# Attention probabilities in tiles of 4 heads by 32 queries, turned by VectorE, with score matmuls on four 64x64 quadrants

## The chip, the core and the metric

The kernel runs on one core of a Trainium2 chip. The metric is device time in microseconds (us), the median of several executions. Five engines work from queues of their own, each in its written order, and signal each other by semaphores: TensorE (PE, matmuls; PEld is its weight load), VectorE (DVE), ScalarE (ACT), GpSimd (POOL) and SyncE (SP), which here only issues DMAs.

## The reference, cut to what matters

The program is one transformer-like layer over 32 sequences of 128 tokens with 128 channels, in fp32. A mixture of 8 experts with a shared one feeds an attention with a band of 32 (no softmax), a layer norm and a residual. Then comes the attention that the change touches: 16 heads of 64 channels that share one key and one value, l2-normalised queries and keys, a learnt relative bias, a causal mask, a padding mask and one "null" key. A gated feed-forward network ends it.

```
q  = l2norm(xn @ Wq) * q_scale            # 16 heads x 64
k, v = split(xn @ Wkv)                    # one head of 64, shared
s  = 8 * q @ [null_k, l2norm(k) * k_scale].T + [null_bias, rel_bias + causal + padding]
p  = softmax(s)                           # 128 queries x (1 + 128) keys
z  = (p @ [null_v, v]) @ Wout             # then a layer norm and the feed-forward part
```

Key positions after the query are masked with -1e30, so their probabilities are zero.

## The kernel before, in words

The 32 sequences go in 8 groups of 4 (`GB`). A pass works on three groups at once: stage A of group g+1 (routing, experts, band attention, norms, projection of q, k and v), stage B of group g (the attention with softmax), and stage C of group g-1 (feed-forward). The passes are fill, start, five of "steady", seventh, last and drain. The order of each engine's work in a pass is a table written out by hand (`ORDER`, lines 53 to 193); each item is a step and its number, such as `sim.0`.

Stage B of one group, before:

- `sim.n` (PE, `sim`, L1369), 12 bursts, 3 for each sequence of 6, 6 and 4 heads: q of one head (64 x 128) times the keys (64 x 129), two heads at once on the upper and the lower 64 rows of the array, into two PSUM banks of ring S. A fp32 matmul shows as two records.
- `sim.n` on DVE (`score`, L1131): one instruction a head, 128 x 129, scales by 1/|q| (`rq`) and adds the masked bias. `max.j` (L1139), `ex.j` (ACT, L759), `inv.j` (L1144) and `pn.j` (POOL, L660) follow, with j = 0 to 15 for 4 heads each. `bias.j` (POOL, L653) makes the masked bias of 4 heads.
- `PT.j` (PE, `p_turn`, L1377): four 128x128 transposes into ring T, `PT.j` (ACT, `pt_copy`, L773) copies them to `pT`.
- `PV.n` (PE, `pv`, L1384), 8 a group: v (128 x 64) times the turned probabilities of 4 heads (128 x 512), twice, on the left and the right half of the columns. `PV.n` on ACT (`ot_copy`, L780) copies to `oT`, and `z.n` (PE, L1397) projects.

Stage A ends with the query norms: `qs.c` (PE, `q_sum`, L1351) sums the squares, `ssq` and `ssc` (DVE, with a PE transpose `qst` between them, L1358) bring them to rows, and `qn` (POOL, L643) takes the power -0.5, once for each sequence. `vs` (DVE, L1084) makes v minus the null value.

PSUM has ring M of 3 banks for stages A and C, S of 2, T of 2, and one bank for z.

SP's queue of a steady pass is `rw.0 maskn.0 wb.0 l4.0`: load the x of the next group (`load_x`, `xg` at L549 and `xs` at L551), its mask, the routing weights of the group after (`load_weights`, 8 DMAs, L542, once `l4` of PE has read `hA`), and store a group's result. ACT's and DVE's lists of a pass begin with `xh.0` (L718) and `xl.0` (L1016), which split x into a high and a low part; PE's `exp.0` to `exp.4` (L1255 by way of the helper `three`, L1243) are the first to read them. Then come `down.0` (L1296), `qkv.0` and so on.

## Time and profile before

| | |
|---|---|
| median of 3 runs | 814.14 us (812.65 to 814.35) |
| profiled execution, first to last instruction | 811.5 us |
| PE busy | 777.8 us, 96% |
| PE weight load busy | 593.4 us, 73% |
| ACT, DVE busy | 602.6 us (74%), 581.3 us (72%) |
| POOL busy | 460.3 us (57%) |
| DMA | 23.41 MB, mean 29 GB/s |

The profile gives no time of the execution beyond its span; the median lies 2.6 us above the span. A busy share tells how full an engine is; who sets the end is read from the chain of waits (from the last instruction back to what released it) and from the timeline. Matmul records overlap, so the time that a stretch of matmuls costs is read from the starts, or from the chain, not from the mean of a record. A steady pass takes 93.2 to 93.4 us.

### The profile page before, as it was taken

The numbers are of one execution on the slowest core, as the hardware profiler recorded it, in microseconds if no ns is written. First come the engines' busy times: TensorE is split into PE (matmuls) and PEld (weight loads), VectorE is DVE, ScalarE is ACT, GpSimd is POOL, SyncE is SP. The second block draws the span as 40 slices with busy tenths as digits, with TensorE's granted clock in tenths as the row PEclk, the third lists the DMA queues.
The fourth block names the chain that finished last, engine by engine and source line by source line (L and its number), as shares of the span: only waits on it lengthen the run. The fifth ranks groups of instructions, "written<-read, shape, count | busy, mean of one in ns | idle before, by whom it ended". The sixth has DMA issues, their size and how long they took to land.

```text
span 811.5 us, 16623 instructions
## 1 busy us (share of the span) xinstructions
PE 777.8 (96%) x5322; PEld 593.4 (73%) x5322; DVE 581.3 (72%) x1575; ACT 602.6 (74%) x1647; POOL 460.3 (57%) x388
## 2 busy tenths in 40 slices
...
DMA packets 28917, 23.41 MB, mean 29 GB/s; under 512 B 2192, under 2 KB 26400, under 8 KB 28448
## 3 DMA queue, kind: packets, MB, share of 16 engines
...
q14 instruction: 40, 0.33, 0.1%
...
## 4 chain that ended last, share of the span: by engine, by line
PE 68%; DVE 13%; POOL 7%; issue 5%; ACT 1%; DVEq 0%; POOLq 0%; ACTq 0%
PE ps_M L1243 33%; PE ps_S L1369 6%; PE ps_T L1384 6%; PE ps_z L1397 5%; PE ps_T L1377 5%; DVE sb_sm L1131 5%; PE ps_M L1429 3%; PE ps_M L1296 3%; POOL sb_sm L660 2%; PE ps_S L1351 2%; POOL sb_biasm L653 2%; DVE sb_hT L1043 2%; POOL sb_rq L643 1%; PE ps_M L1326 1%; DVE sb_bs L1033 1%
## 5 line engine op out<-in xcount | busy, mean ns | idle before, releaser
L660 POOL TENSOR_TENSOR sb_sm<-sb_sm,sb_rden 128x512 f32<-128x512 f32 x128 | 146.2, 1145 | 155.6 <-DVE sb_rden L1144 155.6
L759 ACT ACTIVATE sb_sm<-sb_sm,sb_nmx 128x129 f32<-128x129 f32 x512 | 200.1, 397 | 28.4 <-DVE sb_nmx L1139 28.0
L653 POOL TENSOR_TENSOR sb_biasm<-sb_bias,sb_maskn 128x512 f32<-128x512 f32 x128 | 168.8, 1326 | 57.3 <-DVE sb_sm L1131 36.7
L1131 DVE SCALAR_TENSOR_TENSOR sb_sm<-ps_S,sb_rq,sb_biasm 128x129 f32<-128x129 f32 x512 | 141.0, 345 | 24.0 <-PE ps_S L1369 20.1
L643 POOL TENSOR_TENSOR sb_rq<-sb_qss,sb_mhalf 128x16 f32<-128x16 f32 x32 | 93.2, 2938 | 21.9 <-DVE sb_qss L1116 21.9
L759 ACT ACTIVATION_READ_ACCUMULATOR sb_sm<-sb_sm,sb_nmx 128x1 f32 x512 | 99.1, 193 | 0.0
L1369 PEld LDWEIGHTS ps_S<-sb_k,sb_qs 64*128 64x128 f32 x1024 | 65.2, 187 | 40.7 <-issue 38.4
L773 ACT ACTIVATE sb_pT<-ps_T 128x512 f32<-128x512 f32 x128 | 74.8, 593 | 26.8 <-PE ps_T L1377 26.8
L1139 DVE TENSOR_REDUCE sb_nmx<-sb_sm 128x4 f32<-128x516 f32 x128 | 86.2, 682 | 1.4
L1369 PE MATMUL ps_S<-sb_k,sb_qs 64*128 64x129 f32 x1024 | 83.0, 291 | 3.8 <-DVE sb_sm L1131 2.2
L1377 PE MATMUL ps_T<-sb_ident,sb_sm 128*128 128x128 f32 x512 | 77.1, 276 | 3.7 <-POOL sb_sm L660 3.5
L1377 PEld LDWEIGHTS ps_T<-sb_ident,sb_sm 128*128 128x128 f32 x512 | 59.6, 141 | 22.4 <-POOL sb_sm L660 10.7
L1397 PE MATMUL ps_z<-sb_wout,sb_oT 128*128 128x128 f32 x512 | 66.9, 276 | 0.0
L1384 PE MATMUL ps_T<-sb_pT,sb_vs 128*64 128x512 f32 x256 | 64.9, 610 | 0.0
L1397 PEld LDWEIGHTS ps_z<-sb_wout,sb_oT 128*128 128x128 f32 x512 | 62.8, 192 | 2.7 <-issue 0.8
L1090 DVE TENSOR_SCALAR sb_qs<-ps_M,sb_cols 128x512 f32<-128x512 f32 x62 | 45.4, 745 | 23.2 <-ACT sb_hT L747 16.9
L1243 PE MATMUL ps_M<-sb_hAh,sb_h1h 128*128 128x512 f32 (+1 forms) x144 | 56.2, 390 | 1.1 <-DVE sb_hAl L959 0.9
L1243 PE MATMUL ps_M<-sb_hBh,sb_h2h 128*128 128x512 f32 (+1 forms) x144 | 55.9, 388 | 0.5 <-DVE sb_hBl L959 0.5
L1144 DVE RECIPROCAL sb_rden<-sb_den 128x4 f32<-128x4 f32 x128 | 21.8, 171 | 46.5 <-ACT sb_sm L759 46.4
L713 ACT ACTIVATE sb_gs<-ps_M 128x512 f32<-128x512 f32 x39 | 23.2, 595 | 41.2 <-PE ps_M L1243 41.1
L1243 PE MATMUL ps_M<-sb_hAh,sb_h1l 128*128 128x512 f32 (+1 forms) x144 | 53.2, 370 | 0.0
L1243 PE MATMUL ps_M<-sb_hAl,sb_h1h 128*128 128x512 f32 (+1 forms) x144 | 53.2, 369 | 0.0
...
## 6 DMA issues: line engine op xcount, KB each, us to landing
...
sb_xg<-in_xT SPq DMA_DIRECT2D x8, 256.0 KB, 4.1
sb_xs<-in_x SPq DMA_DIRECT2D x8, 256.0 KB, 4.6
sb_qs<-in_xT SPq DMA_DIRECT2D x1, 2048.0 KB, 10.2
sb_hA<-in_h SPq DMA_DIRECT2D x2, 1024.0 KB, 5.2
out_y<-sb_res SPq DMA_DIRECT2D x7, 256.0 KB, 3.9
sb_sm<-toeplitz SPq DMA_DIRECT2D x1, 1024.0 KB, 5.8
...
```

The costliest lines, as they stand in the source:

```text
L643: pool.tensor_tensor(rq[:, cut], qss[:, cut], mhalf[:], ALU.pow).then_inc(q_rnorm.sem, 1)
L653: pool.tensor_tensor(biasm[:, heads, 1:NK], bias0[:, heads], maskn[:, j // 4].unsqueeze(1).broadcast_to([128, 4, S]), ALU.add)\
L660: pool.tensor_tensor(sm[:, heads, 1:NK], sm[:, heads, 1:NK], rden[:, heads].unsqueeze(2).broadcast_to([128, 4, S]), ALU.mult)\
L759: ins = act.activation(sm[:, h], sm[:, h], ACT.Exp, bias=nmx[:, h:h + 1], accum_out=den[:, h:h + 1])
L773: act.activation(pT[:, heads].rearrange("p h s -> p (h s)"), bank(g, "PT", j)[:], ACT.Copy)\
L1131: ins = dve.scalar_tensor_tensor(sm[:, h], bank(g, "sim", n, odd)[:, m * NK:(m + 1) * NK], rq[:, k * HEADS + h:k * HEADS + h + 1], biasm[: ...
L1139: dve.tensor_reduce(nmx[:, heads], sm[:, heads], AX, ALU.max, negate=True).then_inc(max_ready.sem, 1)
L1243: ins = pe.matmul(ps, w[i], x[j], start=start and n == 0, stop=stop and n == 2)
L1369: ins = pe.matmul(ps[odd][:, m * NK:(m + 1) * NK], qs[half, lo + m, k * S:(k + 1) * S], k2[half, k], start=True, stop=True)
L1377: ins = pe.transpose(ps[:, h * S:(h + 1) * S], sm[:, j % 4 * 4 + h, 1:NK], ident[:])
L1384: ins = pe.matmul(ps[DH * odd:DH * (odd + 1)].rearrange("p (h s) -> p h s", h=4), vs[:, n // 2], pT[:, n % 2 * 8 + odd:n % 2 * 8 + 8:2], s ...
L1397: ins = pe.matmul(zbank[:, k * D:(k + 1) * D], oT[:, c], wout[:, c], start=(c == 0), stop=(c == NP - 1))
```

## The change

It touches stage B and what feeds it.

- Scores are tiled as 4 heads x 32 queries = 128 partitions. A query block i (0 to 3) needs keys up to 32(i+1) only, so tiles are 33, 65, 97 and 129 wide (`WIDE`); `sim`, the bias, the maxima, the exponentials, the division and the PV product skip the masked keys beyond. Units come in the order of `BLOCKS` 0, 3, 1, 2, two to a burst; there are 2 bursts a sequence instead of 3.
- `sim.n` (PE) issues 16 matmuls a burst of 64 rows x 64 columns, over the four quadrants of the array (`half` and `part`), instead of 6 or 4 of 64 rows x 128 columns.
- The PE transposes `PT`, their copies on ACT and ring T go. `tp.j` on DVE (`p_turn`) turns the probabilities in 32x32 blocks, straight into `pT`.
- After such a turn a column holds (head, key) pairs of four heads, so PV multiplies with `vblk`, a block form of v: rows of a 32-key block repeated for 4 heads, 64 rows of the array for a pair of heads, 128 columns. 14 matmuls a sequence of 256 or 128 columns stand for 4 of 512.
- `vblk` is filled by 16 DMAs a group on SP (`vb.0`, `spread_values`), which wait until `vs` is made and until the last PV of the group before has read the old one.
- The query norms are summed in 8 matmuls of 512 columns, turned by DVE from PSUM (the transpose `qst` goes).
- The first bias load from DRAM is 16 DMAs instead of one, and 4 small ones come before the expert weights.
- PSUM: ring S has 4 banks, shared by `sim`, `qs` and PV. All order tables are new.

```diff
-BURSTS = ((0, 3), (3, 6), (6, 8))
-NB = len(BURSTS)
-LAST_BURST = (0, 1, 1, 2)
+QW = 32
+BLOCKS = (0, 3, 1, 2)
+PAIRS = (BLOCKS[0:2], BLOCKS[2:4])
+NB = len(PAIRS)
+WIDE = [QW * (i + 1) + 1 for i in range(4)]
+TURNED = 5 * 128
+RING = 3
...
     "sp steady": """
-        rw.0 maskn.0 wb.0 l4.0
+        rw.0 maskn.0 wb.0 l4.0 vb.0
     """,
...
-BANKS = {"M": 3, "S": 2, "T": 2}
+BANKS = {"M": 3, "S": 4}
...
+            def spread_values(g, k):
+                sp.wait_ge(v_shifted.sem, v_shifted.at(g, 1))
+                if g == 0:
+                    sp.wait_ge(v_cleared, 1)
+                sp.wait_ge(pv_psum.sem, pv_psum.at(g, 0))
+                for i in range(4):
+                    for c in range(4):
+                        sp.dma_start(vblk[c * QW:(c + 1) * QW, :, i, c % 2 * DH:(c % 2 + 1) * DH], vs[i * QW:(i + 1) * QW])\
+                            .then_inc(v_spread.sem, 16)
...
+            def p_turn(g, j):
+                n, (i, wide, _) = j // 2, unit(j % 4)
...
+                dve.wait_ge(p_normed.sem, p_normed.at(g, j + 1))
+                dve.wait_ge(pv_psum.sem, pv_psum.at(g, n + 1 - RING))
+                p = scored(g, j)[:, :, 1:wide].rearrange("p t (c k) -> p t c k", k=QW)
+                turned = pT[:, (g * GB * NB + n) % RING].rearrange("p (c t k) -> p t c k", t=4, k=QW)
+                if i == 2:
+                    dve.transpose(turned[:, :, 1:4:2], p[:, :, 0:2])
+                    ins = dve.transpose(turned[:, :, 4:5], p[:, :, 2:3])
...
             def sim(g, n):
-                k, (lo, hi) = n // NB, BURSTS[n % NB]
...
-                        ins = pe.matmul(ps[odd][:, m * NK:(m + 1) * NK], qs[half, lo + m, k * S:(k + 1) * S],
-                                        k2[half, k], start=True, stop=True)
+                for i in PAIRS[n % NB]:
+                    for m in range(2):
+                        for c in range(2):
+                            for odd in range(2):
+                                half, part = slice(64 * odd, 64 * odd + 64), slice(64 * c, 64 * c + 64)
+                                ins = pe.matmul(ps[odd][part, first:first + WIDE[i]],
+                                                qs[half, m, 4 * k + i, 2 * c:2 * c + 2].rearrange("p c q -> p (c q)"),
+                                                k2[half, k, 0:WIDE[i]], start=True, stop=True)
...
             def pv(g, n):
...
-                for odd in range(2):
-                    ins = pe.matmul(ps[DH * odd:DH * (odd + 1)].rearrange("p (h s) -> p h s", h=4), vs[:, n // 2],
-                                    pT[:, n % 2 * 8 + odd:n % 2 * 8 + 8:2], start=True, stop=True)
+                for c in range(hi + 1):
+                    both = c <= lo
+                    for r in range(2):
+                        half = slice(64 * r, 64 * r + 64)
...
+                        src = pT[half, ring, first:first + (256 if both else 128)]
+                        ins = pe.matmul(dst, vblk[half, k, c], src, start=(c == 0), stop=(c == hi), skip_group_check=True)
```

Where things now stand. SP's queue between two steady passes, first before and then after: `sb_xg` and `sb_xs` are the x of the next group, `in_mask` its mask.

```order
L542 DMA sb_hA<-routes 64x4x128 x8
L566 DMA out_y<-sb_res 128x4x128
L549 DMA sb_xg<-in_xT 128x512
L551 DMA sb_xs<-in_x 128x4x128
L558 DMA sb_mask<-in_mask 128x512
```

```order
L567 DMA sb_hA<-routes 64x4x128 x8
L601 DMA out_y<-sb_res 128x4x128
L594 DMA sb_vblk<-sb_vs 32x4x64 x16
L574 DMA sb_xg<-in_xT 128x512
L576 DMA sb_xs<-in_x 128x4x128
```

Sixteen DMAs that wait for the last PV of the group now stand between the store and the load of x.

PE's queue over the same boundary, from the last PV (L1384, L1440) to the first matmul that reads the new x (`sb_xh`), first before: L1358 turns the sums of squares, L1397 is z, L1369 the scores.

```order
L1384 MATMUL ps_T<-sb_pT,sb_vs 64x512 x2
L1358 MATMUL ps_S<-sb_ident,sb_ssT 128x128
L1397 MATMUL ps_z<-sb_wout,sb_oT 128x128 x8
L1369 MATMUL ps_S<-sb_k,sb_qs 128x129 x6
L1243 MATMUL ps_M<-sb_xh,sb_wguh 128x512
```

The same of the changed kernel: L1453 is z, L1377 a transpose of k, L1402 the sums of squares, L1416 the scores.

```order
L1440 MATMUL ps_S<-sb_pT,sb_vblk 128x256 x4
L1440 MATMUL ps_S<-sb_pT,sb_vblk 128x128 x2
L1453 MATMUL ps_z<-sb_wout,sb_oT 128x128 x4
...
L1453 MATMUL ps_z<-sb_wout,sb_oT 128x128 x4
L1377 MATMUL ps_M<-sb_ident,sb_hT 128x128 x4
L1402 MATMUL ps_S<-sb_hT,sb_heads 32x512 x2
L1402 MATMUL ps_S<-sb_gs,sb_heads 32x512 x2
L1453 MATMUL ps_z<-sb_wout,sb_oT 128x128 x12
L1416 MATMUL ps_S<-sb_k,sb_qs 64x33 x8
L1416 MATMUL ps_S<-sb_k,sb_qs 64x129 x8
L1416 MATMUL ps_S<-sb_k,sb_qs 64x65 x8
L1416 MATMUL ps_S<-sb_k,sb_qs 64x97 x8
L1294 MATMUL ps_M<-sb_xh,sb_wguh 128x512
```

What is left out in the middle are the nine matmuls of `q.5` to `q.7`. Before, one burst of scores stood between the last z and the experts; now two do.

## Rows read from the trace of the kernel before

**Rows 1.** Page, part 1: busy us, share of span, instructions.
```profile
PE 777.8 (96%) x5322; PEld 593.4 (73%) x5322; DVE 581.3 (72%) x1575; ACT 602.6 (74%) x1647; POOL 460.3 (57%) x388
```
**Rows 2.** Busy by stretch: start pass, a steady pass, last pass; header names the columns.
```profile
core 0: us, PE busy (x) PEld busy (x) DVE busy (x) ACT busy (x) POOL busy (x), PEclk, DMA share, GB/s
72.50:143.70 71.20, 63.93 (x484) 45.04 (x483) 60.35 (x162) 54.37 (x176) 57.20 (x43) 1.00 0.13 39
330.40:423.60 93.20, 91.98 (x629) 69.84 (x630) 69.13 (x185) 72.34 (x200) 56.98 (x45) 1.00 0.08 22
702.40:811.50 109.10, 103.04 (x730) 84.75 (x728) 54.87 (x147) 89.34 (x226) 36.76 (x35) 1.00 0.03 8
```
**Rows 3.** Chain of waits, 300 to 420 us: start, us, engine, line, records.
```profile
309.65 0.72 PE ps_S L1369 x8
...
323.38 0.44 PE ps_T L1377 x4
...
324.25 0.89 PE ps_z L1397 x8
325.14 0.71 PE ps_M L1243 x3
...
326.29 1.01 PE ps_S L1351 x32
327.30 1.01 PE ps_T L1384 x4
328.31 0.26 PE ps_S L1358
...
330.36 0.87 PE ps_S L1369 x12
...
340.71 4.53 PE ps_M L1296 x10
...
357.81 1.87 PE ps_T L1384 x8
```
**Rows 4.** Timeline of SP in the fill and at a pass boundary.
```profile
4.68 0.43 SPq L494 DMA_DIRECT2D sb_pb<-in_pb  x1
5.15 0.42 SPq L494 DMA_DIRECT2D sb_maskn<-in_wqkv  x1
5.62 0.44 SPq L506 DMA_DIRECT2D sb_xs<-in_x  x1
...
36.90 0.33 SPq L515 DMA_DIRECT2D toeplitz<-sb_pT  x1
38.35 0.38 SPq L517 DMA_DIRECT2D sb_sm<-toeplitz  x1
...
410.97 5.20 SPq L542 DMA_DIRECT2D sb_hA<-routes  x8
416.22 0.86 SPq L566 DMA_DIRECT2D out_y<-sb_res  x1
417.12 0.50 SPq L549 DMA_DIRECT2D sb_xg<-in_xT  x1
```
**Rows 5.** DMA issues: KB each, us from issue to landing.
```profile
sb_xg<-in_xT SPq DMA_DIRECT2D x8, 256.0 KB, 4.1
sb_sm<-toeplitz SPq DMA_DIRECT2D x1, 1024.0 KB, 5.8
sb_maskn<-in_wqkv SPq DMA_DIRECT2D x1, 192.0 KB, 5.5
```
**Rows 6.** Timeline of ACT and DVE where a steady pass begins.
```profile
422.14 0.62 ACT L718 ACTIVATE sb_xh<-sb_xg 128x512 fp32r<-128x512 f32 x1
...
422.80 0.69 DVE L1016 TENSOR_TENSOR sb_xl<-sb_xg,sb_xh 128x512 fp32r<-128x512 f32 x1 [0.43 <-ACT sb_xh L718]
425.17 1.65 DVE L1131 SCALAR_TENSOR_TENSOR sb_sm<-ps_S,sb_rq,sb_biasm 128x129 f32<-128x129 f32 x6 [0.27 <-POOL sb_rq L643]
432.48 0.69 DVE L1139 TENSOR_REDUCE sb_nmx<-sb_sm 128x4 f32<-128x516 f32 x1
435.73 0.68 DVE L1002 TENSOR_TENSOR sb_hT<-ps_M,sb_gs 128x512 f32<-128x512 f32 x1
```
**Rows 7.** Timeline of PE in the fill: an idle stretch and the same matmuls after it.
```profile
53.42 0.66 PE L1281 MATMUL ps_M<-sb_ident,sb_hA 128*128 128x128 f32 x2 [4.30 <-DVE sb_hT L1043]
53.87 3.62 PE L1237 MATMUL ps_S<-sb_sm,sb_pT 128*128 128x512 f32 x4
...
58.99 0.61 PE L1326 MATMUL ps_M<-sb_ident,sb_hT 128*128 128x128 f32 x4
...
60.33 1.02 PE L1237 MATMUL ps_S<-sb_sm,sb_pT 128*128 128x512 f32 x2
```
**Rows 8.** Instructions of DVE, ACT by line and shape: busy us, mean ns, idle.
```profile
L1162 DVE SCALAR_TENSOR_TENSOR sb_al<-ps_M,sb_cols,sb_al 128x512 f32<-128x512 f32 x28 | 21.0, 751 | 14.6 <-ACT sb_al L794 11.8 <-PE ps_M L1243 2.8
L1162 DVE SCALAR_TENSOR_TENSOR sb_al<-ps_M,sb_cols,sb_al 128x256 f32<-128x256 f32 x8 | 3.9, 482 | 4.8 <-ACT sb_al L794 4.4 <-PE ps_M L1243 0.3
L773 ACT ACTIVATE sb_pT<-ps_T 128x512 f32<-128x512 f32 x128 | 74.8, 593 | 26.8 <-PE ps_T L1377 26.8
```
**Rows 9.** Timeline of DVE in the fill and where the start pass begins.
```profile
5.18 0.54 DVE L858 TENSOR_TENSOR sb_pT<-sb_condT,sb_wgT 64x256 f32<-64x256 f32 x1 [3.06 <-DMA sb_wgT<-in_wgT]
...
71.23 0.41 DVE L1084 TENSOR_TENSOR sb_vs<-sb_hT,sb_rows 128x256 f32<-128x256 f32 x1
...
74.99 1.65 DVE L1131 SCALAR_TENSOR_TENSOR sb_sm<-ps_S,sb_rq,sb_biasm 128x129 f32<-128x129 f32 x6 [0.78 <-POOL sb_rq L643]
```
**Rows 10.** POOL instructions by line and shape: busy us, mean ns, idle.
```profile
L653 POOL TENSOR_TENSOR sb_biasm<-sb_bias,sb_maskn 128x512 f32<-128x512 f32 x128 | 168.8, 1326 | 57.3 <-DVE sb_sm L1131 36.7 <-DVE sb_maskn L1097 20.5
L660 POOL TENSOR_TENSOR sb_sm<-sb_sm,sb_rden 128x512 f32<-128x512 f32 x128 | 146.2, 1145 | 155.6 <-DVE sb_rden L1144 155.6
L643 POOL TENSOR_TENSOR sb_rq<-sb_qss,sb_mhalf 128x16 f32<-128x16 f32 x32 | 93.2, 2938 | 21.9 <-DVE sb_qss L1116 21.9
```

More of the change, by code:

```diff
@@ L70 @@
+        mix.0 z.0 l3.0-2 sim.6-7 xnT.0 l3.3 z.1 kv.0 q.0-1 PV.2-4 q.2-3 l4.0 q.4 z.2 PV.5 qs.0-3 PV.6-7 z.3
+        q.5-7 z.4 kT.0 qs.4-7 z.5-7
     """,
     "pe seventh": """
-        exp.0 sim.0 exp.1-2 sim.1 exp.3 sim.2 exp.4 down.0 zT.0 PT.0 sim.3 PT.1 qkv.0 l1.0-1 PT.2 l1.2-3 sim.4
-        PV.0 scores.0 PT.3 sim.5 l2.0 PT.4 z.0 PT.5 sim.6 mix.0 PV.1 sim.7 PT.6 l2.1 PT.7 PV.2 sim.8 l2.2 PT.8
-        z.1 PT.9 z.2 sim.9 l2.3 PT.10 xnT.0 PV.3 sim.10 l3.0 kv.0 q.0 PT.11 q.1 sim.11 PV.4 q.2-3 l3.1 z.3 PT.12
@@ L138 @@
-        max.7 inv.6 sim.6 max.8 inv.7 mix.0 sim.7 inv.8 max.9-10 ln1.0 inv.9 sim.8 max.11 h2.0 inv.10 sim.9
-        ln2.0 h2.1 inv.11 max.12 xnT.0 h2.2-3 sim.10 max.13 maskn.0 kv.0 q.0-1 max.14 inv.12 sim.11 q.2 inv.13
-        max.15 inv.14 q.3 inv.15 q.4 kT.0 q.5 ssq.0 q.6 vs.0 ssc.0 q.7
+        xl.0 ln3.0 sim.0 exp.0-3 max.0 sim.1 max.1-3 exp.4 sim.2 zT.0 down.0 inv.0-1 zl.0 tp.0 max.4 inv.2 max.5
+        tp.1 qkv.0 scores.0 inv.3 sim.3 max.6 l1.0 tp.2 l1.1 h1.0-1 l1.2 inv.4 max.7 l1.3 mix.0 tp.3 h1.2-3
```

386 lines of the change are left out of this document (206 added, 180 removed).

## The prediction

> **What bounds the kernel now.** I read the busy shares first: PE 96%, the next engine 74% [rows 1]. Then the busy time by stretch: in a steady pass PE is busy 91.98 of 93.20 us, DVE 69.13, ACT 72.34, POOL 56.98 [rows 2]. Then the chain of waits, which gives what a burst really costs on PE, since records overlap. Sixteen PT of 0.44, eight bursts of scores at 0.87 and four at 0.72, eight PV at about 0.98 (1.87 a pair, 1.01 alone), eight z at 0.89 [rows 3], and the 108 fp32r matmuls of 512 columns at 0.23 to 0.24 each (0.71 for three) add up, with the rest, to some 90 us of a pass of 93.2. So PE's work sets the steady passes. In the start pass it doesn't: PE is busy 63.93 of 71.20 and DVE 60.35 [rows 2]. The last pass is PE's again (103.04 of 109.10), with ACT at 89.34.
>
> **The change part by part.** *PE, per steady pass.* The transposes go: 16 x 0.44 = 7.0, and the turn of the sums, 0.26 [rows 3]. Scores were 8 x 0.87 + 4 x 0.72 = 9.8. Now they are 8 bursts of 32 records, of 64 weight columns and a mean width of 81 on four quadrants. No row shows four quadrants. The nearest row with four independent parts of the array is the sums of squares, 32 records of 128 columns in 1.01, 32 ns each; the other end is the pace of today's scores on two halves, 0.87/12 = 73 ns. That gives 1.01 or 2.32 a burst; I take 1.05, because the parts are four and the widths smaller than in the row of 1.01. So 8.4, a gain of 1.4; at the other end a loss of 8.8. PV was 7.8. Now each sequence has 12 records of 256 columns and 16 of 128, on two halves of 64 rows. Two sharing PV records of 512 columns take 1.87/8 = 0.234 each, so 0.117 for 256; for 128 columns with 128 weight columns in two halves today's scores are the same case, 0.073. 12 x 0.117 + 16 x 0.073 = 2.57, times 4 = 10.3, a loss of 2.5 (1.5 if the narrow ones take half of 0.117). The sums of squares keep their columns and save about 0.2. Sum: -7.0 - 0.3 - 1.4 + 2.5 - 0.2 = **-6.4 a pass**.
>
> Here a rule of the Trainium skill speaks against the change: "TensorEngine Tiling (Array Packing)", Instruction Overhead, says that a matmul has an overhead of some 60 cycles and that tiling gains nothing along a dimension that is already small. Its estimate for the 33-wide scores would be 60 columns' worth instead of 33 for half of the records of half of the bursts, some 0.4 us a pass or 3 in the whole. No row here has so narrow a matmul.
>
> *DVE, per pass.* Scores are as many but 48 columns narrower in the mean. From 482 to 751 ns for 256 to 512 columns [rows 8] a column costs 1.05 ns: 64 x 0.05 = -3.2. Maxima, 16 instructions 192 columns narrower: -3.2. New are 20 turns over 5120 columns. Not shown before; plain instructions give 5.4 by the slope and 0.07 to 0.15 each to start, 6.8 to 8.4; a turn could be up to twice as slow a column (+5), and hardly cheaper. The turn of the sums from PSUM adds 0.4. Net +0.8 to +2.4 on 69 us: DVE stays behind PE, and I price it at nothing in the steady passes because PE covers it. The skill's "Vector Engine (DVE) Microarchitecture Reference", section 3.8, has such a turn sustain one element per cycle and lane, which would make the 5120 columns about as dear as a plain instruction's.
>
> *ACT and POOL.* ACT loses the copies, 74.8 us in all [rows 8], and some 20 of narrower exponentials. POOL's two big groups lose 3/8 of their columns, some 100 of 315 us [rows 10]. Neither is what the steady passes wait for, so I give them no gain there; in the last pass they only follow PE.
>
> *SP.* This is the step that decides. SP issues in strict order. Its queue has sixteen DMAs for `vblk` between the store and the load of the next x, and the first waits for the last PV of the pass. Issues back to back start 0.47 us apart (4.68, 5.15, 5.62) and the eight 64-partition ones 0.65 (5.20/8) [rows 4]. I take 0.50: 8.0 us from the end of PV.7 (call it T) to the issue of x. Then 4.1 to land [rows 5], `xh` 0.62, `xl` 0.69 [rows 6] and 0.25 for hand-overs: x is split at T + 13.7. PE's work after PV.7 is z.3, three q, z.4, kT, four qs, three z: 0.89 + 2.1 + 0.89 + 0.44 + 0.9 + 2.67 = 7.9, and two bursts of scores, 2.1: it stands at T + 10.0. So PE idles 3.7. In the kernel before x was issued at 417.12, 6 us before the pass began, and PE never waited for it. Behind the wait DVE is late too, since `xl.0` is first in its list and `sim.0`, `exp.0` follow: from `xl` to the last `hidden` it has 1.5 (stats) + 2 x 1.8 (scores) + 4 x 1.4 + 0.6 (experts) + 0.9 (two maxima) = 12.2, and `down` ends 0.9 later, 13.1; PE alone would need 7.0 + 4.5 = 11.5. That is 1.6 more. And a halted PE comes back slow: after 4.30 us idle four records took 3.62 us where two take 1.02 [rows 7], half the clock, the lower of its two levels (1.2 GHz); I add 0.4, since DVE is the later one there. Together **+5.7 at each of the five boundaries into passes 2 to 6**, between 3.5 (issues at 0.40, no slow clock) and 8.5 (0.65).
>
> At the boundary into pass 1, `vb.0` is followed by the eight `wb.0` (5.2) before the load: x is split at T + 18.9, PE stands at T + 7.7; with the same 2.1: **+13.3**.
>
> *Fill and start.* Four small DMAs put the load of wqkv 1.9 later, at 7.1, landing at 12.6 [rows 4, 5]. ACT's first and DVE's second item wait for it, and the first expert routing (DVE L858, 5.18 before [rows 9]) stands behind. I let the chain of routing and experts absorb most of it. The bias then goes to DRAM only after `scores.0` of PE, at about 49 by my count from the lists; 1.45 later its 16 loads, 7.0 apart from first to last, and 5.8 to land, give 62 to 63 for the flips; PE has them ahead of `xnT`, which began at 58.99 [rows 7]. Stage B thus starts 5.3 later. Then x of group 1 is behind 16 `vblk` DMAs that need `vs`: split at about 90, while DVE's first scores ran at 74.99 [rows 9]. From 90 on, DVE has some 58 us of its 60.35 to do, and I add 3 for waits: the start pass ends at 152 to 153 instead of 143.7: **+9** (2 if POOL's powers, 2.9 each [rows 10], done meanwhile, give it a better run; 16 if not).
>
> **Sum.** Passes 2 to 6: 5 x (-6.4 + 5.7) = -3.5. Pass 1: -6.4 + 13.3 = +6.9. Last: -6.4. Fill and start +9. Together +6.0 on the span of 811.5, 817.5; with the 2.6 by which the median lies above the span, **820 us**. The gain of the matmuls is eaten by a load of x that comes late.
>
> **Rivals.** *A, x is not late.* Should sixteen small DMAs issue in 0.2 us each, or PE reach the experts later for other reasons, the boundaries cost nothing: 8 x -6.4 = -51, fill and start +5, so 768. For it: PE-bound passes at 96%. Against: no issue in the trace is shorter than 0.33. *B, faster by half*: issues near 0.40 and a start pass that catches up, 5 x -3 - 6.4 + 5 + 2, near 797. *C, the quadrants don't overlap*: scores at 73 ns a record, +8.8 instead of -1.4: 10.2 more in each of 8 passes, about 900. It decides from 45 ns on, where the gain of the transposes is gone. For it: weight loads of 64 columns are twice as many. Against: the row of 1.01. *D, DVE becomes the bound on the slower side.* DVE's turns wait in order for POOL's division, with scores and expert steps queued behind them; at 1.5 us of such waits a pass, or turns at double price, PE idles some 2 to 3 more in each pass: 835 to 845.
>
> **How the numbers follow.** Chances: forecast 0.50 (its own range 803 to 838, of which a sixth is below 812.5 and a tenth within), A 0.17, B 0.15, C 0.06, D 0.12. About 0.2% is what a measurement of this kernel can tell from no change. Faster: 0.17 + 0.15 + 0.08 = 0.40; same 0.05; slower 0.55. Both signs have much of it, so the range for 8 in 10 runs from 772, which takes in part of A, to 848, beyond D; outside are most of A and all of C.
>
> **What would show each step.** In the profile of the changed kernel: no L1377-like transposes of probabilities; 32-record bursts of scores at 1.0 to 1.1; PV of a sequence near 2.6; turns on DVE at 0.3 to 0.6; SP's sixteen issues taking 8 us, then `xg`, and ACT's `xh` waiting for a DMA 3 to 6 us at the start of each of six passes, with PE idle and its clock down; steady passes of 92 to 93 us. A steady pass of 87 with no such wait would make it A; score bursts over 1.5 us, C.

## The result, and the profile after

The changed kernel takes 831.22 us (median of 4 runs, 828.2 to 831.59) against 813.57 us of the kernel before, run beside it (812.65 to 814.35). The ratio is 1.021, 95% interval 1.0191 to 1.0229: 17.7 us slower. The profiled execution took 828.2 us with a span of 826.5; before, the span was 811.5.

The page of the changed kernel, part 1 and PE's clock in 40 slices (tenths of full speed):

```profile
PE 720.0 (87%) x6080; PEld 576.1 (70%) x6080; DVE 575.9 (70%) x1735; ACT 520.1 (63%) x1519; POOL 356.9 (43%) x395
...
PEclk9799699969999899989999999989998899999999
```

Every engine has less to do than in [rows 1]: PE 57.8 us less, ACT 82.5, POOL 103.4. The work went down and the time went up, so the time is in waits. The clock row shows where: it dips in the slices of six of the seven pass boundaries (not at 455 us), and once in the fill. The stretches of the first two steady passes and of the last two passes together:

```profile
core 0: us, PE busy (x) PEld busy (x) DVE busy (x) ACT busy (x) POOL busy (x), PEclk, DMA share, GB/s
177.10:270.00 92.90, 84.97 (x722) 67.60 (x722) 68.53 (x205) 61.92 (x184) 40.53 (x44) 0.96 0.11 27
270.00:362.50 92.50, 84.63 (x722) 67.35 (x722) 68.49 (x205) 61.92 (x184) 43.18 (x45) 0.96 0.11 28
640.50:826.50 186.00, 177.31 (x1554) 146.82 (x1554) 124.39 (x391) 140.43 (x398) 69.03 (x79) 0.99 0.03 9
```

Against [rows 2] a steady pass has 7.3 us less of PE's work, some of it at the lower clock, and is only 0.7 shorter. What stands between is seen on SP. Its queue from the end of pass 1:

```profile
252.32 0.60 SPq L601 DMA_DIRECT2D out_y<-sb_res  x1
254.49 10.71 SPq L594 DMA_DIRECT2D sb_vblk<-sb_vs  x16
265.25 0.59 SPq L574 DMA_DIRECT2D sb_xg<-in_xT  x1
```

The sixteen `vblk` DMAs start with the end of the last PV (253.05 + 1.35, below) and hold x back by 10.8 us. In [rows 4] x was issued right behind the store. PE over the same boundary:

```profile
253.05 1.35 PE L1440 MATMUL ps_S<-sb_pT,sb_vblk 64*128 64x256 f32 x12 [0.82 <-DVE sb_pT L1189]
...
262.91 1.47 PE L1416 MATMUL ps_S<-sb_k,sb_qs 64*64 64x33 f32 x64
...
270.02 0.80 PE L1294 MATMUL ps_M<-sb_xh,sb_wguh 128*128 128x512 f32 x1 [5.64 <-DVE sb_xl L1050]
270.61 0.63 PE L1294 MATMUL ps_M<-sb_xl,sb_wguh 128*128 128x512 f32 x1
...
274.00 0.40 PE L1294 MATMUL ps_M<-sb_xh,sb_wguh 128*128 128x512 f32 x1
274.24 0.40 PE L1294 MATMUL ps_M<-sb_xl,sb_wguh 128*128 128x512 f32 x1
```

PE has 10.0 us of work from the last PV to the end of two bursts of scores (264.38), then idles 5.64 until x is split. The first matmuls after it come 0.43 us apart, later ones 0.23. The granted clock is 0.50 from 270 to 274 us, the lower of the two levels (1.2 GHz), and 1.00 in the 4 us behind: some nine matmuls at half pace, 1.8 us lost. The split on DVE waits 7.63 us here, and 13.44 and 17.24 at the first two boundaries:

```profile
96.54 0.69 DVE L1050 TENSOR_TENSOR sb_xl<-sb_xg,sb_xh 128x512 fp32r<-128x512 f32 x1 [13.44 <-ACT sb_xh L758]
...
176.39 0.69 DVE L1050 TENSOR_TENSOR sb_xl<-sb_xg,sb_xh 128x512 fp32r<-128x512 f32 x1 [17.24 <-ACT sb_xh L758]
...
269.27 0.69 DVE L1050 TENSOR_TENSOR sb_xl<-sb_xg,sb_xh 128x512 fp32r<-128x512 f32 x1 [7.63 <-ACT sb_xh L758]
```

To compare kernels I use one mark: the start of PE's first expert matmul (`xh` times `wgu`) in each pass. All times in us, from the timelines of PE.

| first expert matmul of | before | changed | difference |
|---|---|---|---|
| fill | 21.31 | 31.00 | +9.7 |
| start pass | 74.83 | 97.29 | +22.5 |
| pass 1 | 144.70 | 177.14 | +32.4 |
| pass 2 | 237.94 | 270.02 | +32.1 |
| seventh pass | 609.95 | 640.47 | +30.5 |
| end of the span | 811.5 | 826.5 | +15.0 |

The kernel loses 32.4 us by pass 1, gains 0.4 a pass in the five steady ones, and wins 15.5 back in the last two, neither of which has a load of x at its end.

### The profile page after: what moved, and what is told of

Same layout as the page of the kernel before. It is cut to its first block and busy times, and to the rows that moved or that the text cites. A ratio compares the mean times of both kernels' runs of the same rounds, so it can differ in the third digit from the quotient of the medians.

```text
span 826.5 us, 18078 instructions
## 1 busy us (share of the span) xinstructions
PE 720.0 (87%) x6080; PEld 576.1 (70%) x6080; DVE 575.9 (70%) x1735; ACT 520.1 (63%) x1519; POOL 356.9 (43%) x395
## 5 line engine op out<-in xcount | busy, mean ns | idle before, releaser
L701 POOL TENSOR_TENSOR sb_sm<-sb_sm,sb_rden 128x128 f32<-128x128 f32 (+3 forms) x128 | 97.1, 764 | 230.5 <-DVE sb_rden L1177 230.4
L800 ACT ACTIVATE sb_sm<-sb_sm,sb_nmx 128x65 f32<-128x65 f32 (+3 forms) x512 | 178.2, 352 | 16.5 <-DVE sb_nmx L1173 16.1
L1166 DVE SCALAR_TENSOR_TENSOR sb_sm<-ps_S,sb_rq,sb_biasm 128x65 f32<-128x65 f32 (+3 forms) x512 | 112.2, 292 | 9.6 <-PE ps_S L1416 8.0
L693 POOL TENSOR_TENSOR sb_biasm<-sb_bias,sb_maskn 128x128 f32<-128x128 f32 (+3 forms) x128 | 109.1, 871 | 15.9 <-DVE sb_sm L1166 11.8
L1440 PE MATMUL ps_S<-sb_pT,sb_vblk 64*128 64x128 f32 (+1 forms) x896 | 83.3, 329 | 6.5 <-DVE sb_pT L1189 6.1
L1440 PEld LDWEIGHTS ps_S<-sb_pT,sb_vblk 64*128 64x128 f32 x896 | 70.1, 188 | 25.3 <-issue 11.1
L1453 PEld LDWEIGHTS ps_z<-sb_wout,sb_oT 128*128 128x128 f32 x512 | 62.9, 192 | 9.5 <-issue 6.0
L1453 PE MATMUL ps_z<-sb_wout,sb_oT 128*128 128x128 f32 x512 | 67.4, 279 | 0.0
L1173 DVE TENSOR_REDUCE sb_nmx<-sb_sm 128x4 f32<-128x132 f32 (+3 forms) x128 | 58.7, 474 | 0.1
L812 ACT ACTIVATE sb_oT<-ps_S,sb_cols 128x512 f32<-128x512 f32 x64 | 43.3, 680 | 22.7 <-PE ps_S L1440 14.1
L1294 PE MATMUL ps_M<-sb_hBh,sb_h2l 128*128 128x512 f32 (+1 forms) x144 | 53.4, 371 | 0.0
L1294 PE MATMUL ps_M<-sb_hBl,sb_h2h 128*128 128x512 f32 (+1 forms) x144 | 53.2, 369 | 0.0
## 6 DMA issues: line engine op xcount, KB each, us to landing
sb_qs<-in_xT SPq DMA_DIRECT2D x1, 2048.0 KB, 10.8
```

What stands on the lines that cost most here:

```text
L693: pool.tensor_tensor(masked_bias(j % 4)[:, :, 1:wide], relative(bias0, i), maskn[:, j // 4, 0:wide - 1].unsqueeze(1).broadcast_to([128, 4, ...
L701: pool.tensor_tensor(p, p, stat(rden, g, j).unsqueeze(2).broadcast_to([128, 4, wide - 1]), ALU.mult)\
L800: ins = act.activation(p[:, t], p[:, t], ACT.Exp, bias=least[:, t:t + 1], accum_out=total[:, t:t + 1])
L812: act.activation(half, bank(g, "PV", n // 2 * 2, n % 2)[:].rearrange("p (i t q) -> p i t q", i=4, t=4), ACT.Identity, bias=nval).then_inc( ...
L1166: ins = dve.scalar_tensor_tensor(scored(g, j)[:, t], bank(g, "sim", n, odd)[:, first:first + wide], rq[:, col:col + 1], masked_bias(j % 4) ...
L1173: dve.tensor_reduce(stat(nmx, g, j), scored(g, j), AX, ALU.max, negate=True).then_inc(max_ready.sem, 1)
```

## Experiments

Two theories stood at the start. **L**: the matmul work did shrink as meant, and the late x eats it. **Rivals**: the stalls have another cause (DVE's list, the fill, the quadrants), or something else becomes the bound once x is early.

### x first

```diff
     "sp fill": """
-        vb.0 maskn.0 rw.0 hw.0 wr.0
+        rn.0 vb.0 maskn.0 hw.0 wr.0
     "sp start": """
-        maskn.0 rw.0 hw.1 vb.0 wb.0
+        maskn.0 hw.1 rn.0 vb.0 wb.0
     "sp steady": """
-        rw.0 maskn.0 wb.0 l4.0 vb.0
+        maskn.0 wb.0 l4.0 rn.0 vb.0
```

`rn` is `load_x` for the group after next. The same load now stands directly ahead of `vb.0` at the end of a pass's list, where it stood directly behind it at the head of the next.

> The changed kernel with one order changed on SP: the load of the next x is issued before the sixteen loads of vblk, in the fill, the start pass and every steady pass. Theory L (the late x is what eats the gain): the waits of 13.4, 17.2 and 7.3 to 8.8 us of DVE for xh at the seven boundaries go, with PE's idle 12.5, 14.9 and 5.3 to 7.3 us and its half clock after them (about 2 us each); steady passes fall from 92.5 to 85.0, the boundary into pass 1 gives back 17, the start pass about 8 of its 12.5, since the powers of the query norms on POOL stand there too: 831 - 37 - 17 - 8 = 769 us. Rival (a bound behind it: DVE's list or the vblk loads, now later, become the wait): PE then idles at PV.0 or at the scores instead, steady passes stay at 89 or more, 795 us or more.

Measured: 781.21 us, ratio 0.960 (0.9588 to 0.9617), 50 us faster than the changed kernel. Passes 2 to 4 take 85.3 us and DVE waits 0.7 for `xh`. L holds for the steady passes to 0.3 us. The total is 12 above the expectation, and one pass has it: pass 1 took 96.5, 11.2 more than the passes behind it. The waits of 158 to 200 us in this kernel name the next in the queue:

```profile
DVE sb_hT L1032 <- DMA sb_hA<-routes: 9.8, 1, 9.8
PE ps_M L1294 <- DVE sb_gs L1023: 9.5, 1, 9.5
```

These are the routing weights of group 2 (`wb.0`), eight DMAs that still stood behind `vb.0` in the start pass.

### x first only in the fill and the start pass

The new order of the fill and the start pass as above; in the steady passes the old one.

> The same order as in x_first, but only for the x of groups 1 and 2 (issued in the fill and in the start pass); the five steady passes keep the sixteen loads of vblk ahead of x. Theory L: the first two boundaries give back 17 + 8, the other five nothing: 806 us, and the distance to x_first is 5 x 7.5 = 37. Rival (the stall of the steady boundaries is PE waiting for DVE for other reasons): the distance to x_first is under 15.

Measured: 822.11 us (ratio 1.010, 1.007 to 1.0131). The distance to `x_first` is 40.9 where 37 was expected: 8 us for each of five boundaries. Of the 25 expected from the first two boundaries 18.0 were back at the mark of pass 1 (159.10 against 177.14). Pass 1 then lost 11.0 of them: it had the same wait for the routing weights (9.4 us), and x late at its end again, with PE idle for 7.1 us. In all 9 were left.

### The weights first too

```diff
     "sp start": """
-        maskn.0 hw.1 rn.0 vb.0 wb.0
+        maskn.0 hw.1 rn.0 wb.0 vb.0
```

> x_first with one more step moved on SP: in the start pass the eight loads of the routing weights stand ahead of the sixteen loads of vblk too. In x_first pass 1 took 96.5 us where the later ones take 85.3, with DVE 9.8 us at a wait for these weights. Theory: the same mechanism a second time, pass 1 falls to 85.5 and the whole from 781 to 770 us. Rival (the weights' load is late for another reason, such as its own wait for h2): pass 1 stays above 92.

Measured: **767.47 us**, ratio 0.944 (0.9405 to 0.9478): 46 us faster than the kernel before and 64 faster than the changed one, with the same instructions in another order on SP. Pass 1 takes 85.67. A steady pass of it:

```profile
239.60:324.90 85.30, 83.02 (x727) 65.79 (x723) 68.54 (x206) 61.81 (x184) 43.12 (x45) 1.00 0.12 30
```

The clock is 1.00 and PE is busy 97%, as in [rows 2], but the pass is 7.9 shorter.

### The same sixteen DMAs in the kernel before

```diff
+            def spread_values(g, k):
+                sp.wait_ge(v_shifted.sem, v_shifted.at(g, 1))
+                sp.wait_ge(pv_psum.sem, pv_psum.at(g, 0))
+                for i in range(4):
+                    for c in range(4):
+                        sp.dma_start(spare[i, c].rearrange("p (b d) -> p b d", b=GB), vs[i * 32:(i + 1) * 32])\
+                            .then_inc(v_spread.sem, 16)
...
-        rw.0 maskn.0 wb.0 l4.0
+        rw.0 maskn.0 wb.0 l4.0 vb.0
```

DVE also waits until the DMAs have read `vs` before it writes the next one; in the start pass `vb.0` stands ahead of `wb.0`, as in the changed kernel.

> The kernel before with sixteen extra DMAs of the size of the vblk loads (32 partitions x 4 x 64 of vs, to DRAM, read by nobody) at the place on SP that they have in the changed kernel, with the same waits. Nothing else is changed, the result too is the same. Theory L by its own formula: x is split 15.6 us after the end of the last PV, where PE has only 2.9 us of other work left (one turn of sums, two z, a burst of scores), so it idles 12.7 and loses about 1.5 by the clock: +14 at five boundaries, +22 into pass 1 (eight more DMAs are ahead), +14 in the start pass: 920 us. Rival (the queue's order costs little, the stall of the changed kernel comes from its other edits): under +40, below 855 us.

Measured: 907.55 us, ratio 1.1155 (1.1136 to 1.1173). PE and SP at one boundary:

```profile
270.66 7.29 SPq L569 DMA_DIRECT2D spare<-sb_vs  x16
278.00 0.42 SPq L551 DMA_DIRECT2D sb_xg<-in_xT  x1
...
271.76 0.94 PE L1382 MATMUL ps_S<-sb_k,sb_qs 64*128 64x129 f32 x12
282.61 0.79 PE L1256 MATMUL ps_M<-sb_xh,sb_wguh 128*128 128x512 f32 x1 [9.91 <-DVE sb_xl L1028]
```

The queue alone costs the kernel before 94 us, where nothing of its compute changed: passes of 105.1 instead of 93.2. It costs more than in the changed kernel because PE there has 2.9 us of work in hand after the last PV, not 10.0. The expectation was 12 too high, and the row says why: these DMAs, to DRAM, took 0.46 each, not 0.67, so x came 3.5 sooner. With that the formula gives 15.6 - 3.5 - 2.9 = 9.2 of idle; the row has 9.91.

### What the issue costs, and fewer of them

The price of an issue was the number that I had wrong. Four kernels with x as late as in the changed one:

```diff
+                sp.dma_start(v_dram.rearrange("p (b d) -> p b d", b=GB), vs[:]).then_inc(v_stored.sem, 16)
+                sp.wait_ge(v_stored.sem, v_stored.at(g, 16))
                 for i in range(4):
                     for c in range(4):
-                        sp.dma_start(vblk[c * QW:(c + 1) * QW, :, i, c % 2 * DH:(c % 2 + 1) * DH], vs[i * QW:(i + 1) * QW])\
+                        sp.dma_start(vblk[c * QW:(c + 1) * QW, :, i, c % 2 * DH:(c % 2 + 1) * DH],
+                                     v_dram[i * QW:(i + 1) * QW].rearrange("p (b d) -> p b d", b=GB))\
```

That is `bounce`: vs goes to DRAM once and the sixteen loads read it there. `bounce4` has one load for each c with all four key blocks i:

```diff
+                for c in range(4):
+                    src = bass.AP(tensor=v_dram.tensor, offset=0,
+                                  ap=[[GB * DH, QW], [DH, GB], [QW * GB * DH, 4], [1, DH]])
+                    sp.dma_start(vblk[c * QW:(c + 1) * QW, :, :, c % 2 * DH:(c % 2 + 1) * DH], src)\
```

`vb_narrow` and then `vb_one` cut the sixteen loads from SBUF themselves:

```diff
+                        sp.dma_start(vblk[c * QW:(c + 1) * QW, :, i, c % 2 * DH:c % 2 * DH + 16], vs[i * QW:(i + 1) * QW, :, 0:16])\
...
+                        sp.dma_start(vblk[c * QW:(c + 1) * QW, 0:1, i, c % 2 * DH:(c % 2 + 1) * DH], vs[i * QW:(i + 1) * QW, 0:1])\
```

> The changed kernel, x as late as there, with vs stored once to DRAM and the sixteen loads of vblk taken from DRAM, same sizes and place. It tells what sets the price of an issue, 0.67 to 0.73 us for these and 0.46 for sixteen of this size that only had DRAM at one end (the bias loads and the extra ones of before_vb). Theory (SBUF at both ends makes the issue dear): 0.5 + 3 of waiting + 16 x 0.46 = 10.9 us from the last PV to x, as now, so 831 us within 5. Rival (32 partitions of SBUF as target and four runs of 256 bytes each set it): 16 x 0.69 + 3.5, x 3.5 later at seven boundaries, 855 us.

> The changed kernel, the load of x as late as there, but vs is stored to DRAM once and vblk filled by 4 loads a group instead of 16, each of 32 partitions x 4 x 4 x 64 (512 runs of 256 bytes instead of 128). Theory I (a price for each issue, 0.7 us or a little over): x is issued 0.5 + 3 + 4 x 0.7 = 6.3 us after the last PV instead of 10.9, so 4.6 earlier at seven boundaries, and PE's clock no longer falls: 831 - 7 x 5 = 796 us. Theory R (the price is by the runs that one issue describes, four times as many here): 4 x 2.6 + 3.5 = 13.9 us, x 3 later, 850 us.

> The changed kernel with each of the sixteen loads of vblk cut from 64 to 16 channels: 128 runs of 64 bytes instead of 256. Three quarters of v are left out of the computation. If the issue's price goes by runs or by the issue it stays 0.67 us each and the time 831; if by bytes it falls towards 0.43, x comes 3 to 4 us earlier at each boundary: 805 us.

> The changed kernel with each of the sixteen loads of vblk cut from four sequences to one: 32 runs of 256 bytes instead of 128. v of three sequences of four is left out of the computation. If the price goes by runs (the extra DMAs of before_vb, whose targets in DRAM are 32 runs of 1 KB, took 0.46 each): 0.43 to 0.46 each, x 3.5 us earlier at each boundary, 803 us; if by the issue: 0.67 each, 831 us.

Measured: bounce 848.54 us (ratio 1.0439, 1.0413 to 1.0464), bounce4 **792.96** (0.974, 0.9695 to 0.9785), vb_narrow 832.27 (1.0226, 1.0183 to 1.0269), vb_one 827.94 (1.0173, 1.0116 to 1.0230; its two runs were 825.3 and 830.6). SP's timeline at the end of pass 1, vb_one:

```profile
256.35 10.79 SPq L594 DMA_DIRECT2D sb_vblk<-sb_vs  x16
267.19 0.58 SPq L574 DMA_DIRECT2D sb_xg<-in_xT  x1
```

and bounce4:

```profile
243.50 0.32 SPq L594 DMA_DIRECT2D v_dram<-sb_vs  x1
247.01 2.65 SPq L599 DMA_DIRECT2D sb_vblk<-v_dram  x4
249.71 0.62 SPq L576 DMA_DIRECT2D sb_xg<-in_xT  x1
```

A quarter of the bytes (vb_narrow) or of the runs (vb_one) makes no issue cheaper: the sixteen took 12.15 at this boundary in vb_narrow, 10.79 in vb_one, 10.71 in the changed kernel. Four times the runs in one issue cost the same 0.66 (2.65/4). So theory I holds: for these loads the price goes by the issue. bounce4 with a quarter of them brings the issue of x to 6.2 us after the store of vs (6.3 expected) and PE's idle at this boundary from 5.6 to 1.4 (0.7 to 2.4 at the five), and it is faster than the kernel before with the order on SP unchanged. bounce pays its detour through DRAM in full: x about 3 later, steady passes 95.5 instead of 92.5. Its loads took 0.64 each from DRAM, so the rival held: SBUF at both ends is not what makes the issue dear. Each microsecond by which x is later is a microsecond of the pass. Why sixteen issues to DRAM, sixteen of the bias (0.47 each, 7.46 in all) or the single loads of the fill (0.43) are cheaper than these stays open.

The Trainium skill, page "DMA: Bandwidth & Descriptors", section "Issuing engines are not separate DMA queues", says that the sequencer's time to initiate a DMA is usually small relative to the DMA itself. This trace differs: a load of `vblk` lands 1.9 us after its issue begins, and 0.67 of that is the issue itself; with sixteen in a row the issues take 10.7 us, and what stands behind them waits for all of it.

### The fill

`fill_order` moves the split of wqkv (`ph.0`) and the routing of the later groups (`lg`, `rx.1`, `rt.5`) behind the first experts; ACT and PE:

```diff
-        ph.0 wh.0 xh.0 rx.0 pb.0 ph.1-2 pb.1 rw.0 exp.0-3 rx.1 exp.4 pb.2 down.0
+        wh.0 xh.0 rx.0 pb.0 pb.1 rw.0 exp.0 ph.0 exp.1 ph.1-2 exp.2 rx.1 exp.3-4 pb.2 down.0
...
-        lg.0 warm.0-5 lg.1-6 pb.0 rw.0 lg.7 pb.1 exp.0-4 down.0 pb.2 warm.6
+        lg.0 warm.0-5 pb.0 lg.1 pb.1 lg.2 rw.0 exp.0 lg.3 exp.1 lg.4-5 exp.2 lg.6-7 exp.3-4 down.0 pb.2 warm.6
```

`x_wb_bias` is x_wb with that, and with the network of the bias between the first experts too; PE:

```diff
-        lg.0 warm.0-5 lg.1-6 pb.0 rw.0 lg.7 pb.1 exp.0-4 down.0 pb.2 warm.6 qkv.0 scores.0 pb.3 warm.7 mix.0
+        lg.0 warm.0-5 pb.0 lg.1 pb.1 lg.2 rw.0 exp.0 lg.3 exp.1 pb.2 lg.4 exp.2 pb.3 lg.5-7 exp.3-4 down.0 warm.6 qkv.0 scores.0 warm.7 mix.0
```

> The changed kernel with the fill's lists of PE, DVE and ACT put nearer to those of the kernel before: the split of wqkv and the routing of the later groups no longer stand ahead of the first experts. Theory: the first PE matmul moves from 12.8 to about 6 us and the first experts from 31.0 to 22; the chain of the relative bias ends earlier by as much, and nothing absorbs it: 831 - 8 = 823 us. Rival (my step in the prediction: the chain absorbs it, since the flips of the bias wait for a DMA chain that begins elsewhere): the flips stay near 62.8 and the time within 2 us of 831.

> x_wb with the fill's lists changed further: the network of the relative bias runs between the first experts on PE, DVE and ACT, as in the kernel before, and the split of wqkv no longer stands first. Theory: the bias leaves for DRAM at about 38 instead of 52 us, its sixteen loads land before 50, PE no longer waits 7.7 us for them, and the first scores come 6 to 8 us earlier: 763 us. Rival (the fill of the changed kernel has a second chain, LN and projections, just behind): 769 to 771.

Measured: fill_order 830.16 us (1.021, 1.0184 to 1.0236) and x_wb_bias 767.70 (0.943, 0.9408 to 0.9453), each the same as the kernel that it was made from. In fill_order the first experts come at 23.4 instead of 31.0, and x of group 1 is split 1.2 earlier: absorbed. In x_wb_bias the first experts come at 22.6, in x_wb at 27.2; PE no longer waits for the bias (7.83 us in x_wb), but for the layer norm right behind it. PE's wait in the changed kernel, then in x_wb_bias:

```profile
62.81 1.65 PE L1288 MATMUL ps_S<-sb_sm,sb_pT 128*128 128x384 f32 x2 [7.72 <-DMA sb_sm<-toeplitz]
```

```profile
67.87 1.11 PE L1377 MATMUL ps_M<-sb_ident,sb_hT 128*128 128x128 f32 x4 [6.55 <-DVE sb_hT L1077]
```

Both theories of a gain in the fill fell.

### Quadrants or halves

```diff
-                        for c in range(2):
-                            for odd in range(2):
-                                half, part = slice(64 * odd, 64 * odd + 64), slice(64 * c, 64 * c + 64)
-                                ins = pe.matmul(ps[odd][part, first:first + WIDE[i]],
-                                                qs[half, m, 4 * k + i, 2 * c:2 * c + 2].rearrange("p c q -> p (c q)"),
-                                                k2[half, k, 0:WIDE[i]], start=True, stop=True)
+                        for odd in range(2):
+                            half = slice(64 * odd, 64 * odd + 64)
+                            ins = pe.matmul(ps[odd][:, first:first + WIDE[i]],
+                                            qs[half, m, 4 * k + i].rearrange("p c q -> p (c q)"),
+                                            k2[half, k, 0:WIDE[i]], start=True, stop=True)
```

> x_wb with the score matmuls on two halves of the array instead of four quadrants: 8 matmuls of 64 rows x 128 weight columns a burst instead of 16 of 64 x 64, the same widths and results. Theory P (in quadrants the pace is set by the record, 0.83 us for 32 records is 26 ns each however narrow they are): in halves 8 wide records at 73 ns and 8 narrow ones at 26 give about 0.79 a burst, so the same time as x_wb within 3 us. Rival Q (the quadrants do overlap and this is what they gain): 16 records at the 73 ns of the kernel before are 1.17 us a burst, +3.1 a pass, +25 in all.

Measured: 780.14 us (0.9598, 0.9565 to 0.963), 12.7 above x_wb: halfway between the two. The chain of waits (start, us, engine, tile, line, records) of x_wb, then of x_wb_halves, at the start of a steady pass:

```profile
336.57 0.83 PE ps_S L1416 x32
337.99 0.73 PE ps_S L1416 x32
```

```profile
347.24 1.09 PE ps_S L1415 x16
348.92 1.07 PE ps_S L1415 x16
```

A record costs 23 to 26 ns on quadrants and 67 to 68 in halves. Both bursts have 162 keys (33 + 129, 65 + 97), so what the width does is read from the starts of the single records. On quadrants four records start within 20 ns, and the next four 58 ns behind them for 33 and for 65 keys, 83 for 97 and 110 for 129. In halves two start within 7 ns and the next two 112 ns behind them, whatever the width (105 + 7). Eight fours give 4 x 58 + 4 x 110 = 0.67 us, eight pairs 0.90, and the rest of the 0.83 and 1.09 is the way to the next matmul. So quadrants do overlap, and four records with 33 keys cost half of two in halves.

Rival Q has the mechanism and its size is too large: 0.26 to 0.34 us a burst were gained, 2.2 of PE's work a pass, of which 1.7 show in the passes (86.95 against 85.25), where +3.1 was expected. Theory P fell: wide records on quadrants are not as cheap as narrow ones, and narrow ones in halves are not as cheap as on quadrants. The floor below which width doesn't count is 58 ns with 64 weight columns and 112 with 128, and the weight loads of the two kernels point the same way (134 ns and 191 ns a record); that they set it is argued, not shown by a run of its own.

The Trainium skill, "TensorEngine Tiling (Array Packing)", Instruction Overhead, has a matmul of one column cost as much as one of about 60: on quadrants the trace agrees, with the same 58 ns for 33 and 65 keys. In halves the floor reaches to 129 keys. It did not stop the finer tiling from paying.

### How free DVE is

`x_wb_turns2` issues the turns of `p_turn` a second time, after a wait for the first; `x_wb_turns_more` does so for units with i = 3 alone:

```diff
+                if i == 3:
+                    dve.transpose(turned[:, :, i // 3:i // 3 + i + 1], p).then_inc(turned_once.sem, 1)
+                    dve.wait_ge(turned_once.sem, turned_once.at(g, j // 4 + 1))
```

`x_wb_turns_less` turns one key block of these units instead of four, and `before_max` is an edit of `maxima` in the kernel before:

```diff
+                elif i == 3 and g > 0:
+                    ins = dve.transpose(turned[:, :, 1:2], p[:, :, 0:1])
...
+                if j % 4 == 3:
+                    dve.tensor_reduce(nmx[:, heads], sm[:, heads], AX, ALU.max, negate=True).then_inc(twice.sem, 1)
+                    dve.wait_ge(twice.sem, twice.at(g, j // 4 + 1))
```

> x_wb with every 32x32 turn of probabilities on DVE done twice, the second into the same place after a wait for the first. It adds some 8.4 us of DVE's work a pass (67.2 in all by x_first's rows), 68.5 becomes 77 to 78 of 85.3. Theory: PE still sets the pass and covers it, since a free engine shows no wait: at most +2 a pass, below 786 us. Rival D of the prediction (DVE's list is in order, so its work lands on the path long before it is full): +6 to +8 a pass, 825 us or more.

> x_wb with only the four 512-wide turns of a group done twice, each again after a wait: 4 x 0.69 and 4 waits of about 0.1, some 3.1 us more of DVE's work a pass, a third of what x_wb_turns2 added for 9 us a pass. Theory S (in this order of the lists each microsecond of DVE is on the path from the first one): +3 a pass, 767 + 24 = 791 us. Rival (DVE has slack, and the 9 us came only once that was used up): under +8 in all, below 775.

> x_wb with the 512-wide turns cut to 128 columns from the second group on, so that three of the four 32-key blocks of the last query block keep old probabilities: this part of the computation is left out, to see DVE relieved. It takes 4 x (0.69 - 0.25) = 1.8 us of DVE's work from a pass. Theory S: -1.8 a pass, 767 - 12 = 755 us. Rival (PE, busy 83 of 85.3, sets the pass in x_wb): 765 to 768.

> The kernel before with the maxima of one unit in four done twice, the second after a wait for the first: 4 x 0.69 and 4 waits, some 3.1 us more of DVE's work a pass, nothing else. The prediction priced +0.8 to +2.4 of DVE at nothing since PE covers it (91.98 of 93.20 us busy). If that step holds: within 4 us of 813.5. Rival (DVE's list has no slack here either): +3 a pass, 837 us.

| kernel | DVE busy a pass | steady pass | median, us |
|---|---|---|---|
| x_wb_turns_less | 67.1 | 84.9 | 767.24 |
| x_wb | 68.5 | 85.3 | 767.47 |
| x_wb_turns_more | 71.3 | 86.8 | 781.48 |
| x_wb_turns2 | 76.6 | 94.2 | 826.87 |
| before | 69.1 | 93.1 | 813.4 |
| before_max | 72.1 | 95.7 | 826.61 |

(The steady pass is the mean of five, from the marks above; DVE's time is that of a single pass.) The stretches behind three of them, x_wb_turns_more, x_wb_turns2 and before_max:

```profile
332.00:418.60 86.60, 83.30 (x730) 65.81 (x722) 71.33 (x211) 61.96 (x184) 43.11 (x45) 1.00 0.12 30
```

```profile
350.50:443.50 93.00, 85.15 (x727) 67.20 (x722) 76.61 (x226) 61.95 (x184) 43.04 (x45) 0.98 0.11 27
```

```profile
243.60:338.50 94.90, 92.28 (x629) 69.86 (x627) 72.07 (x189) 72.39 (x200) 56.00 (x45) 1.00 0.08 22
338.50:434.90 96.40, 93.76 (x629) 71.06 (x627) 72.13 (x189) 72.37 (x200) 55.98 (x45) 0.98 0.08 21
```

Three microseconds more on an engine that is busy 74% or 80% of the pass cost half to nine tenths of themselves; eight more cost all of themselves; 1.4 less gave 0.4. So my theory fell in x_wb_turns2 and rival D held; in x_wb_turns_more the 14 us lie between S (24) and slack (8); relief gave nothing, as the rival of S has it; and before_max cost 13.2 us, outside the 4 of my step. The point where DVE begins to count is where these kernels stand. With it falls the idea that PE's busy share (97% and 99%) says that another engine is free.

Part of this cost is PE's clock. In before_max the passes at a granted clock of 1.00 took 94.4 to 94.9, 1.7 to 2.1 more than before; the other two (0.98) took 96.4 and 98.1. In x_wb_turns2 all five passes lie at 0.96 to 0.98, and PE is busy 2.9 us more a pass than in x_wb with the same matmuls. Without that, by an estimate from these numbers, three microseconds cost 1.5 to 2 and eight about six.

DVE's work stands in a fixed order, and PE meets it at a few handovers a pass: in the pass of x_wb_turns2 PE waited 4.0 us for turned probabilities and 2.4 for the layer norm; in x_wb the same two waits were 0.8 and 1.5. In before_max the wait for the layer norm rose from 0.7 to 1.9, and a layer norm reads no maxima: there it is the place in the list that counts. The added turns also lengthen the chain from the scores to PV, and for them these runs do not tell the two apart.

## Why the prediction was right or wrong

It said 820 us, slower, by a load of x that comes late; measured were 831.2, slower, by that. The direction and the mechanism held and the range had the time. The size of the loss was wrong: 6 us over the span of before, measured 15.

**PE's work.** Forecast -6.4 a pass; x_wb, without the stalls, shows -7.8 (five passes, 93.05 and 85.25 in the mean). The term that differs is the scores: 1.05 us a burst was taken, 0.83 and 0.73 were measured, 6.2 a pass instead of 8.4. That alone would make it -8.6, and PE's busy time did fall by 8.9; its idle time rose by 1.1, from 1.2 to 2.3. PV is right (2.6 a sequence, 2.57 forecast). Rival C (quadrants don't overlap) is out: 26 ns a record, and four start together.

**SP, the step that was mis-sized.** I took 0.50 us for an issue from rows of other DMAs [rows 4]; these take 0.67 (10.71/16). So x is issued 10.8 after the last PV, not 8.0, and lands in 3.3, not 4.1. At a steady boundary PE idles 5.3 to 7.3, not 3.7, and the lower clock costs 1.8, not 0.4; the 1.6 for DVE doesn't show, `down.0` follows the experts at once. Together 7.4 by x_wb against the changed kernel (92.67 a pass), where 5.7 was forecast. The two errors nearly cancel, which is luck: the five steady passes gained 1.9 us together, forecast 3.5.

**The start pass and its boundaries, where the miss is.** By the mark of pass 1 the forecast was +20.2 (9 + 11.2 of idle), measured +32.4. Of the 12.2, the split of x of group 1 has 7.2: it ended at 97.2, forecast 90. The steps of it are on SP's timeline of the changed kernel:

```profile
77.88 10.71 SPq L594 DMA_DIRECT2D sb_vblk<-sb_vs  x16
88.62 0.60 SPq L513 DMA_DIRECT2D sb_hA<-in_h  x1
89.27 0.43 SPq L554 DMA_DIRECT2D routes<-sb_pT  x1
89.74 0.47 SPq L583 DMA_DIRECT2D sb_mask<-in_mask  x1
90.25 0.91 SPq L574 DMA_DIRECT2D sb_xg<-in_xT  x1
```

`vs` was ready 0.9 later than forecast, the sixteen issues took 2.7 more, three other DMAs of the fill stand between and were not counted (1.7), and x landed in 5.6 instead of 4.1, just behind the load of 1 MB for h1. At the boundary into pass 1 the issues took 11.6 instead of 8: PE idled 14.91, forecast 11.2, 3.7 more. The last 1.3 are in the start pass's own work. So the term that failed is the price of sixteen issues in a row: 8.0 us in the forecast, 10.7 and 11.6 measured. At these two boundaries it makes 6.3 of the 12.2. The rest is what was left out of the start pass's +9: the three DMAs between (1.7), the slower landing (1.5), `vs` (0.9) and the other 1.8.

**The end.** From the mark of the seventh pass on 15.5 us were won, forecast some 10.7 (two passes of 6.4, less the clock and DVE's part at the boundary); the scores again, for the most part. 12.2 + 1.6 - 4.8 = 9.0, which is 826.5 - 817.5.

**Fill.** "The chain of routing and experts absorbs most of it" was right, though the first experts were 9.7 late: fill_order put them 7.6 earlier, and x_wb_bias 4.6 earlier than x_wb, for nothing. The flips came at 62.8, forecast 62 to 63.

**Costed at nothing.** DVE's extra work was priced at nothing, because PE covers it. As a reason that was wrong: before_max shows that there is no such cover. As a number it was nearly right: the net was forecast at +0.8 to +2.4, and the narrower scores and maxima paid for all of the turns, 69.1 us a pass before and 68.5 after. The turns cost 9.1 a pass (8.4 for the probabilities, 0.7 for the sums), forecast 7.2 to 8.8. The timings of the forms in the changed kernel:

```profile
L1193 DVE STREAM_TRANSPOSE sb_pT<-sb_sm 128x512 f32<-128x512 f32 x32 | 22.1, 690 | 9.6 <-POOL sb_sm L701 9.5
...
L1191 DVE STREAM_TRANSPOSE sb_pT<-sb_sm 128x256 f32<-128x256 f32 x32 | 13.8, 432 | 2.3 <-POOL sb_sm L701 2.3
```

690 ns for 512 columns is what a plain instruction of that width takes [rows 6], and from 256 to 512 columns a column costs 1.01 ns, where plain instructions have 1.05 [rows 8]. The Trainium skill, "Vector Engine (DVE) Microarchitecture Reference", section 3.8, has such a turn sustain one element per cycle and lane: the trace agrees, in that a turned column costs no more than a plain one. Rival D (DVE as the bound) didn't decide the changed kernel, but it is the next bound in x_wb, from the first added microsecond. Rival A (x is not late) was what the kernel would be with another order on SP: 768 forecast, 767.5 measured with x and the weights ahead. That they agree so well is luck: by the mark of pass 1 x_wb is 9.2 late, where A has it 1.4 early; the five steady passes gave 39.0 instead of 32.0, the end 17.6 instead of 12.8. What makes the 9.2 is open, as the two runs on the fill found nothing.

**Slips in the sums.** By the prediction's own terms the bounds of a boundary are 3.7 and 8.1, not 3.5 and 8.5; 90 + 58 + 3 is 151, not 152 to 153; rival B comes out near 800, not 797; and the gain of the matmuls is gone at 58 ns a record, not at 45. None of them changes which forecast was made.
